# Ending stage 0 differently: x1 stores on ScalarE's queue, the last chunk's table work behind the first group, block-diagonal input matrices

## Time and profile before

| | us |
|---|---|
| median of three runs | 1714.91 |
| the profiled execution, time | 1716.96 |
| the profiled execution, span of its instructions | 1715.2 |
| stage 0 with what precedes it (to the last L617 matmul) | 257.6 |
| from there to the first matmul of group 0's dense layer | 54.3 |
| group 0 from that matmul to the same one of group 1 | 93.9 |
| the same for group 1 | 87.3 |

### The profile page before, as it was taken

How to read it: one execution, slowest core, us unless ns; L and a number is a source line. 1 busy time by engine, 2 the same in 40 slices (tenths; PEclk the granted TensorE clock), 3 DMA queues, 4 the chain that set the end, 5 groups by cost and what they waited for, 6 DMA issues and landing times.

```text
span 1715.2 us, 30844 instructions
## 1 busy us (share of the span) xinstructions
PE 1577.2 (92%) x12183; PEld 1035.3 (60%) x12183; DVE 1033.8 (60%) x1345; ACT 527.2 (31%) x674; POOL 824.5 (48%) x365
## 2 busy tenths in 40 slices
PE   6767674799999999999999999999999999999996
PEld 6767673356565656575747474747474747474744
DVE  7876767556565656556566666655656565656532
ACT  4433332123232323232323232323232323232311
POOL 2000012535556565656565647474747383838334
PEclk9987878899999999999999999999999999999998
DMA  7798875225353535352526262625252625253314
GB/s 222 269 338 283 323 273 170 62 47 136 72 135 71 135 71 135 69 136 62 143 54 147 51 149 51 147 58 139 66 139 66 139 66 133 72 121 79 79 49 99
DMA packets 425955, 216.81 MB, mean 126 GB/s; under 512 B 337144, under 2 KB 412416, under 8 KB 423872
## 3 DMA queue, kind: packets, MB, share of 16 engines
q1 hardware_dynamic: 413760, 204.19, 45.6%
q10 hardware_dynamic: 12160, 12.14, 2.1%
HBM read 94.19 MB, written 71.76 MB: 97 GB/s over the span
## 4 chain that ended last, share of the span: by engine, by line
PE 82%; DVE 6%; DMA 6%; issue 2%; SPq 1%; ACT 1%; POOL 0%; POOLq 0%; DVEq 0%; ACTq 0%
PE ps L734 39%; PE ps L769 7%; PE ps L672 7%; PE ps L699 6%; DMA arena<-in_x_dram 6%; PE ps L726 5%; PE ps L742 5%; PE ps L782 3%; PE ps L617 3%; PE ps L676 3%; PE ps L716 2%; PE ps L712 1%; PE ps L564 1%; SPq L354 1%; DVE arena L1469 1%
## 5 line engine op out<-in xcount | busy, mean ns | idle before, releaser
L734 PE MATMUL ps<-arena,w2t 128*128 128x512 f16 x3072 | 681.3, 379 | 0.0
L734 PEld LDWEIGHTS ps<-arena,w2t 128*128 128x128 f16 x3072 | 300.6, 98 | 362.5
L532 POOL TENSOR_TENSOR arena<-arena 128x1024 f32<-128x1024 f16 x64 | 151.0, 2360 | 553.3 <-DMA arena<-arena 535.5
L1475 DVE TENSOR_SCALAR arena<-ps,biasx 128x512 f32<-128x512 f32 x128 | 94.4, 748 | 213.9 <-ACT arena L1052 213.8
L1052 ACT ACTIVATE arena<-ps,biasx 128x512 f16<-128x512 f32 x128 | 87.2, 687 | 424.7 <-PE ps L742 424.7
L508 POOL TENSOR_TENSOR arena<-arena 128x1024 f32<-128x1024 f32 x32 | 72.7, 2272 | 298.5 <-DMA arena<-tab_scratch 272.1
L617 PE MATMUL ps<-arena 128*128 128x128 f32 x1024 | 148.9, 312 | 50.9 <-DMA arena<-in_x_dram 43.5
L617 PEld LDWEIGHTS ps<-arena 128*128 128x128 f32 x1024 | 141.9, 225 | 55.7 <-issue 39.3
L699 PE MATMUL ps<-arena 128*128 128x512 f16 (+1 forms) x768 | 137.7, 330 | 18.4 <-DVE arena L1398 17.5
L769 PE MATMUL ps<-arena 128*128 128x256 f16 (+1 forms) x1536 | 137.8, 246 | 3.2 <-DVE arena L1469 3.0
L535 POOL TENSOR_TENSOR arena<-arena,one_xs 128x1024 f32<-128x1024 f32 x64 | 136.0, 2125 | 5.0
(11 more groups left out here) (213 smaller groups left out, 2119.3 us busy)
## 6 DMA issues: line engine op xcount, KB each, us to landing
arena<-in_x_dram SPq DMA_DIRECT2D x64, 512.0 KB, 7.4
out_dram<-arena SPq DMA_DIRECT2D x64, 512.0 KB, 3.0
gbuf<-x_scratch SPq DMA_DIRECT2D x120, 256.0 KB, 3.7
x_scratch<-arena SPq DMA_DIRECT2D x16, 1024.0 KB, 10.3
arena<-krow_scratch SPq DMA_DIRECT2D x32, 512.0 KB, 4.5
x_scratch<-arena SPq DMA_DIRECT2D x16, 896.0 KB, 7.6
arena<-tab_scratch SPq DMA_DIRECT2D x32, 200.0 KB, 2.6
w2t<-in_L_cond_weight_dram ACTq DMA_DIRECT2D x8, 512.0 KB, 3.4
```

What stands on the lines that cost most here:

```text
L532: nc.gpsimd.tensor_tensor(past[:, h % 2].rearrange("p (k t) -> p k t", k=NBLK), x3t[:, h % 2, 0], x3t[:, h % 2, 1], ALU.add).then_inc(past ...
L734: nc.tensor.matmul(ps[:, 4 + o % 3, :], w2t[:, o, part, k, :], xx[:, :, k, :], start=(k == 0 and q == 0), stop=False)
```

## The change

- The input matrices are loaded four times, onto 64 partitions, each pair of copies into its own half of the columns of a `w0n` twice as wide; the other halves are cleared by two VectorE memsets. The one-hot tile now has 64 rows, for even batch rows above and odd ones below. Each product then covers both halves of 64 output rows at once: 64 products instead of 128.
- The x1 stores of units 0 to 6 move from SP to ScalarE's queue, one in each of steps 1 to 4 of the following unit, behind that step's `copy_even`. The last unit's four stay on SP.
- The last loop pass is written out behind the loop (ScalarE, VectorE), so that `combine_a` of the last chunk can be left out of it. `combine_a` otherwise moves from step 6 to step 7, the sines and `sum_k` one step later, and the weight lots of the odd units move forward into the even ones.
- In the stretch for group 0, `near1` and `far1` of row 2 use banks 4 and 5 and row 3 banks 0 and 1; `near1(0, 2)` goes ahead of the second `states`; rows are waited for singly; VectorE's `combine_a` and `combine_b` of the last chunk go behind the last `x2_split_lo`; `sum_k` and the rest go into group 0's dense layer; GpSimd waits for that chunk's tables before it makes those of group 1.

```diff
-            for quarter in range(4):
-                cols = slice(quarter * (C * C // 4), (quarter + 1) * (C * C // 4))
-                sp.dma_start(w0n[0:NID, cols], w0.rearrange("i c d -> i (c d)")[:, cols]).then_inc(w0_loaded, 16)
+            for copy in range(4):
+                q = copy // 2
+                sp.dma_start(w0n[NID * copy:NID * (copy + 1), q * C * C:(q + 1) * C * C],
+                             w0.rearrange("i c d -> i (c d)")).then_inc(w0_loaded, 16)
...
-            STORE_AT = {6: 0, 7: 1, 8: 2, 9: 3}
...
-                    if step in STORE_AT and not (first and k == 0):
-                        store_x1(*((i, 0) if k else (i - 1, 1)), STORE_AT[step])
...
             def body(g, more1):
+                if isinstance(g, int) and g == 0:
+                    pool.wait_ge(tables_ready, NBLK)
                 if more1:
                     make_tables(0, g + 1)
...
-                    for q in range(2):
-                        mm = nc.tensor.matmul(ps[q * C:(q + 1) * C, dgroup, e * PAIRS:(e + 1) * PAIRS], src[:, 8 * dgroup + e, :],
-                                              onehot[:, :].rearrange("i (n q) -> i q n", q=2)[:, q, :], start=True, stop=True)
+                    mm = nc.tensor.matmul(ps[:, dgroup, e * PAIRS:(e + 1) * PAIRS], src[:, 8 * dgroup + e, :],
+                                          onehot[:, :], start=True, stop=True)
...
-                        if step == 1:
+                        if step == 2:
                             sum_k(blk - 1)
...
+                    if isinstance(g, int) and g == 0 and o == 1:
+                        sum_k(NBLK - 1, 3)
+                if isinstance(g, int) and g == 0:
+                    pe.wait_ge(k_scaled, NBLK)
...
             states(0, 0, 0)
+            near1(0, 2)
             states(0, 0, 1)
             states(0, 0, 2)
             for h in range(HG):
-                if h >= 2:
+                if h == 3:
                     near1(0, h)
                 far1(0, h)
-            sum_k(NBLK - 1)
-            pe.wait_ge(k_scaled, NBLK)
...
+            def store_x1(i, half, part):
+
+                act.wait_ge(s0_even_out, (2 * i + half + 1) * (STEPS // 2))
+                act.wait_ge(s0_odd_out, (2 * i + half + 1) * (STEPS // 2))
...
+                    if 1 <= step < 1 + NPART and not (first and k == 0):
+                        store_x1(*((i, 0) if k else (i - 1, 1)), step - 1)
...
+            for q in range(2):
+                nc.vector.memset(w0n[2 * NID * q:2 * NID * (q + 1), (1 - q) * C * C:(2 - q) * C * C], 0.0)
...
-                    if step == 6:
+                    if step == 7 and not (last and k == 1):
                         combine_a(blk, k)
...
-            for h in range(HG):
-                x1_split_lo(0, h)
+            x1_split_lo(0, 0)
             turn_g1(0)
+            x1_split_lo(0, 1)
             bases_lo(0, 0)
+            x1_split_lo(0, 2)
+            x1_split_lo(0, 3)
             table_lo(0, 0)
-            combine_b(NBLK - 1, 1)
             for k in range(NCH - 1):
                 state_lo(0, 0, k)
-            for h in range(HG):
+            take_conv1(0, 0)
+            for h in range(1, HG):
                 take_conv1(0, h)
-                x2_split_lo(0, h)
-            split_k(NBLK - 1)
+                x2_split_lo(0, h - 1)
+            x2_split_lo(0, HG - 1)
+            combine_a(NBLK - 1, 1)
+            combine_b(NBLK - 1, 1)
```

More of the change, by code:

```diff
@@ L309, in row_of, with conv1_bank @@
             return lrow[n % 2 if parity is None else parity]
+        def conv1_bank(g, h):
+            return (0, 2, 4, 0)[h] if isinstance(g, int) and g == 0 else 2 * (h % 2)
         def left_slot(r, n):
@@ L576, in turn_params, with sum_k @@
                 mm.then_inc(params_turned, 1)
-            def sum_k(c):
+            def sum_k(c, bank=4):
                 pe.wait_ge(tables_ready, c + 1)
@@ L635, in stage0 @@
                             turn_lot(LOT_W + 1)
-                        if not first and step == 5:
-                            turn_lot(blk + LOT_W, k)
+                        if not first and k == 0 and step == 3:
+                            turn_lot(blk + LOT_W, 0)
+                        if not first and k == 0 and step == 7:
+                            turn_lot(blk + LOT_W + 1, 1)
             pe.wait_ge(iota_done, 5)
@@ L679, in near1 @@
             def near1(g, h):
-                b0 = 2 * (h % 2)
+                b0 = conv1_bank(g, h)
+                early = isinstance(g, int) and g == 0
                 if h == 0:
                     pe.wait_ge(g1_turned, g + 1)
-                    pe.wait_ge(x1_hi, HG * (g + 1))
-                    pe.wait_ge(x1_lo, HG * (g + 1))
-                if h < 2:
+                if early or h == 0:
+                    pe.wait_ge(x1_hi, HG * g + h + 1 if early else HG * (g + 1))
+                    pe.wait_ge(x1_lo, HG * g + h + 1 if early else HG * (g + 1))
+                if early:
+                    if h == 2:
+                        pe.wait_ge(k_scaled, NBLK - 1)
+                    if h == 3:
+                        pe.wait_ge(c1_out, 1)
+                elif h < 2:
                     at_least(pe, c3_out, HG * (g - 1))
@@ L905, in chunk_sines @@
             def chunk_sines(c, r, step):
-                if step == 2:
+                if step == 3:
                     act.wait_ge(table_angles, 2 * c + 1)
@@ L969, in stage0 @@
                             lot_hi(LOT_W + 1)
-                        if not first and step == 6:
+                        if not first and k == 0 and step == 4:
                             lot_hi(blk + LOT_W)
+                        if not first and k == 1 and step == 0:
+                            lot_hi(blk - 1 + LOT_W + 1)
                         if step == 7:
@@ L976, in _ @@
             stage0(0, True)
-            with act.Fori(1, NBLK // 2) as i:
+            with act.Fori(1, NBLK // 2 - 1) as i:
                 stage0(i, False)
+            stage0(NBLK // 2 - 1, False)
             copy_even(NBLK // 2 - 1, 2 * STEPS - 2)
@@ L1341, in turned_bias, with stage0 @@
                 dve.wait_ge(turned_copied, 1)
-            def stage0(i, first):
+            def stage0(i, first, last=False):
                 for m in range(1, 2 * STEPS, 2):
@@ L1371, in stage0 @@
                             lot_ready(LOT_W + 1)
-                        if not first and step == 4:
-                            lot_ready(blk + LOT_W, k)
-                        if not first and step == 7:
+                        if not first and k == 0 and step == 2:
+                            lot_ready(blk + LOT_W, 0)
+                        if not first and k == 0 and step == 5:
                             lot_lo(blk + LOT_W)
+                        if not first and k == 0 and step == 6:
+                            lot_ready(blk + LOT_W + 1, 1)
+                        if not first and k == 1 and step == 1:
+                            lot_lo(blk - 1 + LOT_W + 1)
                         if step == 5:
@@ L1387, in _ @@
             lot_lo(LOT_W + 1)
[L1388 removed]
+            with dve.Fori(1, NBLK // 2 - 1) as i:
                 stage0(i, False)
+            stage0(NBLK // 2 - 1, False, True)
             copy_odd(NBLK // 2 - 1, 2 * STEPS - 1)
@@ L1478, in body @@
                         lo3(o - 1)
+                    if isinstance(g, int) and g == 0 and o == 1:
+                        split_k(NBLK - 1)
                     if isinstance(g, int) and g == 0 and o >= HG:
```

57 lines of the change are left out of this document (33 added, 24 removed).

## The result

The changed kernel takes 1703.64 us (median of four runs, 1701.11 to 1704.94), beside 1715.93 us for the kernel before on the same chip (1712.47 to 1717.11). The ratio is 0.993, with a 95% interval of 0.991 to 0.9949. The change gains 12.3 us; the forecast was 31.

The account below looks back on a forecast made before the run. TensorE was 82% of the chain, in stage 0 starving for loads queued behind stores. Terms +1.5 - 19 - 5.5 - 9.3 + 1.0 = -31.3 took 1716.96 to 1685.7 us, against the median 1684; range 1666 to 1706.

Parts of the forecast that it names:

- The start: Before stage 0: halved input products gain nothing, one-hot work costs 0.5 and later matrices 1.0 us; +1.5, ends 0 and +7.
- they don't set the end: At the start: input products don't set the end, since VectorE's parameter work delays the first `copy_odd` and bounds unit 0.
- the 42 that I had named as the sign of uncovered memsets: At the start: a first `copy_odd` beyond 42 us would show the memsets uncovered; near 38 was forecast.
- 1.0 of the 2.4 us between my ends: At the start: price for matrices landing as 256 KB pieces, between 0 (5.0 us as before) and 2.4 (7.4 us).
- Stage 0, -19: Units 1 to 7: with stores on ScalarE's queue a unit takes 26.4 us, 2.7 less, times 7: -19 us.
- Waits below 7 us: Stage 0, sign of being right: waits for x loads fall below 7 us, from about 13.5.
- Rival 2: Stage 0: DMA runs at 400 GB/s throughout, 5.1 us less a unit, 36 in all, 1667 us; chance 0.12.
- First half of the transition, -5.5: Last stage 0 matmul to first `far1`: 28 us instead of 33.55, GpSimd starting with that matmul, tables at 14; -5.5.
- Second half, -9.3: First `far1` to group 0's dense layer: GpSimd waits, VectorE runs at full rate, 11.4 us instead of 20.75; -9.3.
- Group 0, +1.0: Group 0's dense layer: `sum_k` lands on a full PE, +1.0 us; GpSimd's tables some 6 us after its start cost nothing.
- 1 (the queue makes no difference): Stage 0: stores and loads compete for the same busy DMA engines, stage 0 keeps its time, 1703 us; chance 0.20.
- 3 (ScalarE blocked by its stores): Stage 0: store issues of 3.4 us hold ScalarE, deciding from 2.2; a unit grows 4.6, 1735 us; chance 0.07.

Follow-up runs that it names:

- experiment 1: The changed kernel with input products, their loads, memsets and one-hot rows as before the change: 1690.48 us, ratio 0.9853 to the kernel before.
- experiment 2: The kernel before the change with only the block-diagonal input products added (their loads, memsets, one-hot rows): 1731.8 us, ratio 1.0094.
- experiment 5: The changed kernel with each input product's 128 weight columns taken from neighbouring elements: products 27.57 us, kernel 1703.05 us.
- experiment 6: The changed kernel with input products using 16 rows instead of 64, still 128 columns: products 28.10 us, kernel 1706.24 us.
- experiment 7: The changed kernel with each input product split into two of 64 columns, output halves in turn, all 64 rows: products 19.01 us, kernel 1692.63 us.
- experiment 8: As experiment 7, but in each group of eight all products of one output half before the other: products 22.96 us, kernel 1700.28 us.
- experiment 9: The changed kernel with each block-diagonal input product done twice: products 55.94 us, kernel 1727.39 us.
- experiment 12: Experiment 1 with the 800 KB table store in step 5 instead of step 2: 1676.82 us, ratio 0.977 to the kernel before.
- experiment 4: Experiment 1 without GpSimd's wait for the last chunk's tables before making those of group 1: 1696.67 us, ratio 0.9886.
- experiment 3: Experiment 1 with the x1 stores of units 0 to 6 issued by SP at their old places: 1700.69 us, ratio 0.9909.

## Why the prediction was wrong, step by step

**The start, "so nothing is gained ... +1.5": the step that failed.** It measured +14.2. Two of its assumptions were false. The first: I counted half as many products as less work for TensorE, hence worth nothing or better, and took no price for them. In fact they take 28.12 us instead of 19.19: a record of 128 weight columns 220 ns, and one of 64, with the halves in turn, 75 (experiments 1, 2, 5 to 9). The rows of before showed the 75 ns in 19.19 us for 256 records, and the line view of before the 344 ns of one: a pace four times shorter than the length means overlap, and whether overlap outlives a new form is not known from it. I should have bounded it. With the 344 ns of one record as the end of no overlap, 128 of them are 44 us, 25 more than before, and my upper end for the start of +7 would have been +32. The claim that "they don't set the end" was false too: with the products over at 44.18 instead of 29.98, stage 0's first matmul follows 1.3 us behind them in both. And VectorE's parameter work, which was to hide them, itself waits for values that ScalarE makes behind copies of the products. So the first `copy_odd` came at 49.28, beyond the 42 that I had named as the sign of uncovered memsets, and it was not the memsets. The second assumption: the matrices land late. I took 1.0 of the 2.4 us between my ends. The profile has 9.0 us to landing, the median of the four, instead of 5.0, above my end of 7.4 for 512 KB, and VectorE had to wait for the last of them:

```profile
arena<-in_L_cond_weights_dram SPq DMA_DIRECT2D x4, 256.0 KB, 9.0
```

They held TensorE up for 5.3 us; how much of that reaches the end, experiment 7 with its one run can't tell (2 us by its times). The memsets, for which I reserved the upper end, were right to the tenth.

**Stage 0, -19: right in direction, too large, its mechanism only in part.** -12.9. I took 26.4 us a unit and counted 2.7 seven times; 26.9 was measured, 2.3 less than before. Over the six distances between waits that makes 13.6, and stage 0 as a whole shows 12.9: ahead of the first wait it lost 2.9 (31.58 from 28.65 us after its start), behind the last it gained 2.2 (20.6 from 22.8). "Waits below 7 us" was wrong (12.8 to 14.2). I had let the loads slip in between single stores. Experiment 12 shows that the place of the table store was a large part of what I missed, but even there waits of 9.4 to 13.7 us remain, so what the loads stand behind stays open. My list of what DMA owes after step 1 had stores and table in it, but I only added their bytes and did not ask whether one could be elsewhere. Rival 2 called 5.1 a unit possible at 400 GB/s; experiment 12 reached 4.4 a unit at 367.

**First half of the transition, -5.5:** -4.5, right in size, wrong in its working. GpSimd began early, and its tables were there at 270.23, 11.3 us after the last matmul, not 14. What follows them took 17.7 us until `far1`, not the 13 that I had added up. Two errors of 3 to 5 us nearly cancelled.

**Second half, -9.3:** -9.9, right with its reason: splits of 1.23, and experiment 4 shows them at 2.07 without the wait. That is 3.9 us of it; what the new banks and the new order give was not tested apart.

**Group 0, +1.0:** +1.0, right; GpSimd began its tables 5.9 us after the dense layer (304.79), and the cover held.

**Rivals.** 1 (the queue makes no difference) is refuted by experiment 3, as far as stage 0 was to keep its time; that its 1703 was met is a coincidence of other terms. 3 (ScalarE blocked by its stores) did not come to its price, for which 4 x 1.2 is 4.8 a unit and not 4.6. The issues of the stores on ScalarE's queue, to be read beside the earlier trace rows:

```profile
L961 ACTq DMA_DIRECT2D x_scratch<-arena x28: 338/357/2089, 71.4 to 241.4; - x28
```

A median of 357 ns against 870 on SP, the longest 2.09, under the 2.2 us from which the rival would decide. The median hides that the store behind the table store took 1.26 to 2.09 in every unit.

## What to carry to other kernels

Halving the count of small matrix products is no saving by itself: divide the stage's time by its records, and where that pace is well below one record's length, price the new form without the overlap as the other bound. When transfers from several queues meet, list all that is in flight in the starved stretch and try to move the one whose user comes last; here that was a table store of 800 KB, worth 13.7 us for one number, more than the 12.3 of the whole change.

## What the hardware showed that I had not expected

- An fp32 product of 64 moving columns has a pace of 74 ns a record with 64 weight columns when the output halves are taken in turn, 90 when they are not, and 215 to 220 with 128 weight columns, whether on 16 or 64 rows, strided or not. That the weight load of the wide one can't run beside the product before it is an explanation that was not tested.
- The granted clock was 1.00 (2.4 GHz) over the whole start, yet the first 32 matmuls of stage 0 took 5.82 us before and 6.04 after, 182 and 189 ns each, and in the kernel before the 24 after them 118 ns each. The row of the clock does not show why.
- The 16 matrices as 256 KB pieces onto 16 partitions each took 9.0 us to land, longer than a 512 KB load of x in the kernel before (7.4).
- A store of the same form took about 0.34 to 0.38 us to issue on ScalarE's queue, and 1.07 to 2.19 when it stood right behind the table store of 800 KB (experiment 1); with the table store moved away none took more than 0.43 (experiment 12). Why is not shown.
